# Three edits to the order of work in the attention layers of a four-part graph network kernel

## What is computed

```python
xw = x @ W
xj = xw[src] + edge_attr @ ew.T + eb
alpha = leaky_relu(att_i . xw[dst] + att_j . xj, 0.2)
ea = exp(alpha - segment_max(alpha, dst)[dst])
alpha = ea / (segment_sum(ea, dst)[dst] + 1e-16)
h = segment_sum(xj * alpha, dst).mean(heads) + b      # relu after the first four
```

## Time and profile before

| | us |
|---|---|
| three runs | 5243.42, 5247.03, 5260.6 |
| median | 5247.03 |
| profiled execution | 5250.73 |
| its span on the core | 5249.0 |
| mean granted clock of PE | 0.882 |
| busy over the span: PE, DVE, ACT, POOL | 4269.4, 4034.0, 3328.7, 3228.0 |
| attention layers in the span | 1571 to 3398 |

### The profile page before, as it was taken

One profiled execution on the slowest core, in us unless ns is written; L12 is line 12 of the kernel. 1 busy time (PEld: TensorE's weight loads), 2 busy tenths in 40 slices (PEclk: granted clock), 3 DMA queues, 4 the chain that ended last, 5 costly groups with the idle time before them and its releaser, 6 DMA issues. The chain is left out here.

```text
span 5249.0 us, 101811 instructions
## 1 busy us (share of the span) xinstructions
PE 4269.4 (81%) x28013; PEld 3696.3 (70%) x28013; DVE 4034.0 (77%) x14947; ACT 3328.7 (63%) x9065; POOL 3228.0 (61%) x2905
## 2 busy tenths in 40 slices
PE   4899999999976978969969959877895868879575
PEld 4777777778866867858858848644775857757475
DVE  5799999999986767767757767687566968859765
ACT  2777777777755857847847848644774547768400
POOL 2888888877777727637457367222752247666277
PEclk6999999999988989989989979955997989989755
DMA  3999997666645646636636546488773759857332
GB/s 91 186 221 221 221 220 221 220 221 207 212 155 127 144 86 132 135 77 142 128 89 141 113 102 148 100 246 239 163 144 85 198 158 246 242 125 134 72 94 85
DMA packets 1107279, 825.55 MB, mean 157 GB/s; under 512 B 209510, under 2 KB 1068202, under 8 KB 1106396
## 3 DMA queue, kind: packets, MB, share of 16 engines
q1 hardware_dynamic: 1026800, 690.47, 50.7%
q0 software_dynamic: 77040, 128.08, 12.7%
q10 hardware_dynamic: 2880, 0.50, 0.1%
HBM read 374.78 MB, written 448.11 MB: 157 GB/s over the span
## 5 line engine op out<-in xcount | busy, mean ns | idle before, releaser
L806 POOL DMA_INDIRECT gat_G<-table,k_src_row x980 | 1072.8, 1095 | 316.5 <-issue 282.2
L1599 ACT ACTIVATE gat_Gw<-gat_G,gat_al 128x128 f32<-128x128 f32 x1960 | 618.5, 394 | 88.9 <-DVE gat_al L1424 88.9
L1455 DVE SCALAR_TENSOR_TENSOR gat_Gw<-gat_own,gat_al,gat_Gw 128x128 f32<-128x128 f32 x1960 | 554.7, 343 | 69.2 <-ACT gat_Gw L1599 69.0
L1716 PE MATMUL gat_psG<-gat_ends_at,gat_Gw 128*128 128x128 f32 x3920 | 538.1, 282 | 43.7 <-DVE gat_Gw L1455 43.6
L1744 PE MATMUL gat_psZ<-gat_aggT,t_gat_wh 128*128 128x256 f32 x1960 | 526.3, 392 | 15.3 <-ACT gat_hT L1625 14.9
L1716 PEld LDWEIGHTS gat_psG<-gat_ends_at,gat_Gw 128*128 128x128 f32 x3920 | 493.4, 197 | 54.9 <-DVE gat_Gw L1455 51.9
L635 PEld LDWEIGHTS nodes_psR<-t_ident_v,nodes_hTl 128*128 128x128 f32 x3168 | 431.7, 192 | 105.5 <-issue 1.8
L635 PE MATMUL nodes_psR<-t_ident_v,nodes_hTl 128*128 128x132 f32 x3168 | 446.1, 278 | 0.0
L479 POOL TENSOR_TENSOR nodes_rstd<-nodes_var,k_half 128x14 f32<-128x14 f32 x140 | 365.7, 2612 | 127.0 <-DVE nodes_var L546 127.0
L1625 ACT ACTIVATE gat_hT<-gat_psZ,t_gat_bias 128x256 f32<-128x256 f32 x490 | 231.1, 472 | 267.4 <-PE gat_psZ L1745 261.9
L1744 PEld LDWEIGHTS gat_psZ<-gat_aggT,t_gat_wh 128*128 128x128 f32 x1960 | 340.1, 194 | 56.1 <-ACT gat_aggT L1606 17.2
(11 more groups left out here) (672 smaller groups left out, 12721.8 us busy)
## 6 DMA issues: line engine op xcount, KB each, us to landing
table<-nodes_rows SPq DMA_DIRECT2D x660, 198.0 KB
table<-nodes_n SPq DMA_DIRECT2D x396, 192.0 KB
gat_own<-table SPq DMA_DIRECT2D x490, 132.0 KB
table<-gat_rows SPq DMA_DIRECT2D x392, 132.0 KB
nodes_x<-in_x SPq DMA_DIRECT2D x132, 192.0 KB
out<-nodes_x_out SPq DMA_DIRECT2D x132, 192.0 KB
gat_G<-table,k_src_row POOLq DMA_INDIRECT x980
hgt_q<-enter_q SPq DMA_DIRECT2D x98, 144.0 KB, 2.2
```

Source lines behind the costliest of these rows:

```text
L806: eng.indirect_dma_start(to, None, table, bass.IndirectOffsetOnAxis(ap=index, axis=0)).then_inc(sem, 16)
L1455: ins = eng.scalar_tensor_tensor(Gw[:, i % RS, t, h, :], own[:, i % RO, t, 0:D], al[:, g % 2, 1, a:a + 1], Gw[:, i % RS, t, h, :], ALU.mul ...
L1599: ins = eng.activation(Gw[:, i % RS, t, h, :], G[:, i % RG, t, 0:D], ACT.Copy, scale=al[:, g % 2, 0, a:a + 1])
L1716: mm = eng.matmul(o[:, h * P:(h + 1) * P], Gw[:, i % RS, t, h, :], ends_at[:, i % RE, t, :], start=True, stop=True)
```

## The change

Three edits in `gat_layer`:

- PE turns the next group's weights (`turn_weights`) as the last thing of its step, behind `mix` and `to_rows`, not right behind `aggregate`.
- ACT may weigh pairs of the next group from the step "take" on, not from one step ahead of "weights".
- At the head of a layer DVE makes `seq4` before it clears the two tiles, and the first eight one-hots before the own scores of groups 0 and 1.

```diff
@@ -1336,8 +1336,6 @@
             @block.vector
             def _(eng):
                 step = Order(eng, s.step)
-                eng.memset(aggE[:, :, 2 * P:4 * P], 0.0).then_inc(s.padded, 1)
-                eng.memset(prE[:, :, :, :, :], 0.0).then_inc(s.zeroed, 1)
                 if l > 0:
                     eng.memset(seq4[:, :], 0.0).then_inc(s.seq, 1)
                     eng.wait_ge(s.seq, 1)
@@ -1345,6 +1343,8 @@
                     eng.wait_ge(s.seq, 2)
                     back = seq4[:, ::-1]
                     eng.tensor_tensor_scan(back, K.q.goes[0:4, ::-1], back, 0.0, ALU.mult, ALU.add).then_inc(s.seq, 1)
+                eng.memset(aggE[:, :, 2 * P:4 * P], 0.0).then_inc(s.padded, 1)
+                eng.memset(prE[:, :, :, :, :], 0.0).then_inc(s.zeroed, 1)
 
                 def source_scores(g):
                     n, p0 = groups[g].pairs, groups[g].first
@@ -1503,10 +1503,10 @@
                     step(eng.tensor_tensor(W0, W0, AS, ALU.mult))
                     eng.tensor_tensor(AS, EL, AS, ALU.mult).then_inc(s.weights, 1)
 
+                for i in range(EARLY):
+                    one_hot(i)
                 own_scores(0)
                 own_scores(1)
-                for i in range(EARLY):
-                    one_hot(i)
                 source_scores(0)
                 scores(0)
                 weights(0)
@@ -1670,7 +1670,7 @@
                         if steps_at(g, k, "scores"):
                             exp(g + 1)
                         for _ in range(2):
-                            if weighed_to < NP and weighed_to <= i + 4 and (at(weighed_to)[0] == g or k >= groups[g].steps["weights"] - 1):
+                            if weighed_to < NP and weighed_to <= i + 4 and (at(weighed_to)[0] == g or k >= groups[g].steps["take"]):
                                 weigh(weighed_to)
                                 weighed_to += 1
                 carried(1, C - P)
@@ -1772,8 +1772,6 @@
                             turn_own(g + 1)
                         if steps_at(g, k, "source"):
                             turn_scores(g + 1)
-                        if steps_at(g, k, "weights"):
-                            turn_weights(g + 1)
                     if i == NP - 6:
                         eng.wait_ge(s.px, P // 2)
                         eng.wait_ge(s.al, NG)
@@ -1796,6 +1794,8 @@
                         mm.then_inc(s.weights_turned, 1)
                     if 2 <= i:
                         to_rows(i - 2)
+                    if i < NP and steps_at(g, k, "weights"):
+                        turn_weights(g + 1)
 
                 eng.wait_ge(s.px, NP)
                 eng.wait_ge(s.pe, NB)
```

## The result

| | before | after |
|---|---|---|
| median of 17 runs each, us | 5244.75 | 5266.31 |
| lowest, highest | 5235.17, 5260.6 | 5247.32, 5286.96 |
| profiled execution, its span | 5250.73, 5249.0 | 5272.63, 5270.9 |
| mean granted clock of PE | 0.882 | 0.878 |

The ratio is 1.0041, 95% interval 1.0029 to 1.0053. The changed kernel is slower by 0.4%, some 21.6 us; 5241 was forecast, 5226 to 5256. In the two profiled executions the attention stage, from the first gather to its last instruction, grew from 1826.2 us to 1841.2, by 15.0.

The account below looks back on a forecast made before the run. PE was taken to bound the attention stage, idle 317 of its 1816 us. Three middle layers at +1.0 us and first and last at +1.4 each gave 5.8, say 6: median 5241 us, range 5226 to 5256.

Parts of the forecast that it names:

- rival 4: Into groups 1, 2 and 3: long stalls cost half-speed stretches and ACT's lead; 19 us slower in all, 5266; chance 0.12.
- a small gain: Whole kernel: the main forecast, some 6 us faster, median 5241, 5229 to 5247 with its bounds; chance 0.52.
- The clock: Half-speed PE stretches behind long stalls: 1.4 us a layer charged into group 2, 0 into 1 and 3, bounds ±1.7.
- Into 3: End of group 2, up to pair 30: aggregate(30) 1.2 us earlier, less 0.65 of debt, net +0.5 us a layer.
- Into 2: End of group 1, to aggregate(16): two waits join, nothing won; chain 0.1 later, debt 0.5, clock 1.4 us lost.
- Into 4, 6 and 7: Ends of groups 3, 5 and 6: gains of 1.5 us into 4 and 1.4 into 6 and 7 together.
- Into 5: End of group 4: turn wait of 0.40 us, a debt of 0.2 remains, net +0.2 us.
- The debt: ACT's lost lead after late weighing makes PE wait once: 0.6 us into group 1, 0.5 into 2, 0.65 into 3.
- The head: Head of a layer: own scores about 3.5 us earlier, but DVE's wait for group 1's gathers absorbs it; 0.
- First and last layer: Late gather waits absorb what is won or lost ahead; only turns into 6 and 7 stay, +1.4 us each.
- stretches at 0.50 in the loops become more by ten or so: PE's half-speed (1.2 GHz) stretches in the attention loops: a sign that the forecast is wrong and the slower rival holds.
- the wait for Gw: PE in the attention stage: a sign of being right, growing from 43.6 us by 20 to 40.

Follow-up runs that it names:

- e3: The kernel before with only the head edit (seq4 and one-hots moved earlier on DVE): 5249.58 us, ratio 1.0009.
- e9: The changed kernel plus eight unused identity matmuls on PE in each stall into groups 1, 2 and 3: 5234.79 us, ratio 0.9966.
- e6: The kernel before with the turn moved everywhere, weighing late only from into group 4 on, old head: 5239.79 us, ratio 0.9999.
- e1: The kernel before with only the weights' turn moved behind mix and to_rows: 5251.11 us, ratio 1.0009.
- e2: The kernel before with only ACT's weighing made late, from the step of the take: 5297.32 us, ratio 1.0100.
- e4: The kernel before with turn and weighing late only from into group 4 on, old head: 5233.03 us, ratio 0.9974.
- e10: The changed kernel with the weights of group 3 alone made one step earlier: 5259.24 us, ratio 1.0005.

## Why the prediction was wrong

**The result is rival 4** (5266, chance 0.12), which says that the long stall is paid in clock and lead. That it met the number to 0.3 us is partly luck: it put 6.9 us a layer into 1, 2 and 3 and left out the 1.2 won ahead of aggregate(30). The middle layers lost 4.2 to 5.2 there, and heads and tails, which it hadn't, 1.4 to 1.8. The forecast of a small gain fails on one step above all.

*The clock.* "Into 3 the fall is there before and after, into 1 too: 0." This step failed. I had one trace, saw one fall into 3 and one into 1, and took the count of falls for fixed. Into 1 the changed order has a lower clock (0.80 for 0.85 in the second layer) and is 1.7 to 2.3 us longer in the middle layers, for which I had charged 0.6 of debt: it ran 11.1 to 12.2 us at 0.50 there, for 8.2 to 8.5 before. Into 3 the comparison was uneven as well. Aggregate(30) itself came as forecast, 9.75 us behind aggregate(28) (2084.64 to 2094.39) for 9.8 forecast and 11.01 before. But the 2076.95 at which aggregate(30) began before already held 2.75 us at a clock of 0.50 (2074.20 to 2076.95), 1.4 of them lost, and my 2075.75 held none. I counted the clock's price as a gain of the edit. Measured at the same clock the order of before takes 45.13 us into 3 (e3, clock 1.00) and the changed one with its idle time filled 45.90 (e9, clock 1.00): 0.8 worse, not 0.5 better. The three middle layers of before all had the fall (46.8 to 47.3), those of e3 none, so even the 0.2 to 0.7 us that the trace shows understates it.

*Into 2* was sized right (signs as in the forecast, plus is a gain): -2.0 forecast, -2.2 measured, with its stretch at 0.50 behind the stall of 2.88 us.

*Into 4, 6 and 7*: +1.5 and +1.4 forecast, +1.2 to +1.5 and +1.2 to +1.3 measured. *Into 5*: +0.2 forecast, between -0.1 and +0.3 measured. *The debt*: 0.5 to 0.65 a group forecast; the changed kernel against e6 gives 0.4 to 1.0 into 1 and 1.1 to 1.4 into 2, at low clocks, and e9 against before 0.6 into 2 at full clock. The price was right there at full speed, and too low where the clock was low.

*The head*: 0 forecast. Alone it is 0 (e3), and some 2 us in five layers were lost in the heads. In the second layer the gather wait of group 1 grew by 3.2 us, for 3.5 forecast (14.93 to 18.09).

*First and last layer.* "What is won or lost ahead of it is absorbed, and only the turns into 6 and 7 stay: +1.4 each." The first layer lost 4.3 instead: what it lost into 1, 2 and 3 (7.9) wasn't absorbed. The last came out at 0.0. Together 7.1 us of the error.

*The tail* wasn't in my sum: 0.9 to 1.3 us longer in four layers, at a clock of 0.79 for 0.93, with the same instructions. But in e3, whose loop and tail are those of before, the three tails took 24.0, 24.5 and 25.1 us, and in e9 23.6, 24.0 and 24.3. So the tail goes with when the clock falls and not with the edit, and its part of the difference may be the luck of the two profiled executions.

In numbers: 3.9, 3.5 and 3.5 us were lost in the middle layers and +1.0 each was forecast, 13.8 us; the first and last layer add 7.1. That is the 20.9 of the stage's difference between forecast (5.8 better) and measurement (15.0 worse). The sign "stretches at 0.50 in the loops become more by ten or so" came as eight. Of the signs of being right, the wait for Gw grew by 47.7 us and not by 20 to 40, and that for alB fell to 37.6 and not below 30, which the 30.5 us at the heads ruled out from the start.

The rows of before held both cases, two short stalls without a fall and two longer ones with it. The Trainium skill ("TensorE: Matmul & The Clock Gate", section "Why this matters for your kernels") advises against idle gaps in TensorE's work because the clock drops back after them, and by it I would have charged all three places. The page speaks of gaps a little longer than those here. In the changed kernel a stretch at 0.50 stands at the stall of 2.8 to 2.9 us at all fifteen places, into 1, 2 and 3 of five layers; but in e1 one such stall of 2.88 us has none, and in e2 two of 2.81 have none (into 2, first and third layer). I gave that reading 0.12 and used it for one place of three.

## What to carry to other kernels

Moving a wait behind ready work gains only if what comes behind the wait is ready too; here the next wait hung on the same chain, so PE's two short stalls joined into one long one, and the clock fell at it more often. Compare positions in a trace only where both ran at the same granted clock, and do not count a fall of the clock as a property of the code when one trace shows it. Where two edits act on the same chain, price them together and apart: late weighing cost 1.0% with the old turn, and 0.3 to 0.4% on top of the moved one.

## What was not expected of the hardware

Matmuls that compute nothing paid for themselves: eight identity products in each of three stalls a layer (16 records, 1.95 us) shortened the stage by 28.9 us in the profiled executions and took the time at 0.50 in the loops from 94.3 to 23.9 us. And the same program order can fall or not: into 2 and into 3, with identical steps, read 1.00 and 0.96 in the kernel before and 0.96 and 1.00 in e3. Counted over the traces, a longer stall only raises the odds of a fall. Into 2, the two short stalls of the old order (1.6 and 0.9 us; kernel before, e3, e4) had a fall at 3 of 15 places; into 3, those of 1.6 and 2.0 us in the same kernels at 10 of 15; the joined stall of 2.88 us into 2 (changed kernel, e1, e6, e10) at 19 of 20. By these odds joining the stalls into 2 costs about 0.75 x 1.7 = 1.3 us a layer, an estimate. What decides at a single place is not settled here.
